# Linear attention and ternary feed-forward on eight cores: the order of three pieces of work at the end of an attention turn

## The reference

```python
# attention half: 16 heads of 64, chunks of 64 tokens, a state S carried from chunk to chunk
qkv = LN(x) @ W_qkv
k   = LN over each head's 64 values
per chunk: inter = S q;  scores = q k^T, causal;  intra = scores v;  S += v k^T;  y = inter + intra
x = x + LN(y @ W_o)
# feed-forward half: activations quantized to 8 bits by row, weights to -1, 0, 1
h = qlinear(layernorm(LN(x), gamma, beta), w1, b1);  h = gelu(h);  h = qlinear(h, w2, b2)
x = x + LN(h)
```

## Time and profile before

| | |
|---|---|
| median of three runs | 3606.48 us (3595.64 to 3606.81) |
| the profiled execution, its own time | 3602.86 us |
| its span, slowest core (core 0) | 3601.3 us (cores: 3567.2 to 3601.3) |
| busy: TensorE (PE), weight load, DVE, ACT, POOL | 58%, 29%, 43%, 20%, 4% |
| DMA | 68 GB/s over the span |

### The profile page before, as it was taken

The page is one execution under the profiler, slowest core; times in us unless marked ns, Lnnn a source line. Parts: engine busy times, 40 slices in busy tenths (PEclk is TensorE's granted clock), DMA queues, the critical chain, the costliest instruction groups (busy, mean ns, idle before and its releaser), DMA issues.

```text
span 3601.3 us, 33831 instructions; the slowest of 8 cores (3567.2 to 3601.3 us)
## 1 busy us (share of the span) xinstructions
PE 2103.5 (58%) x10640; PEld 1032.0 (29%) x10640; DVE 1538.5 (43%) x2492; ACT 726.8 (20%) x1193; POOL 145.9 (4%) x203
## 2 busy tenths in 40 slices
PE   0061566648666366647766366547776366647665
PEld 0041433413222133412222144312222233413222
DVE  0576543345543133345553133445452243355442
ACT  0030321112222111112221112212221121122221
POOL 0141300000000000000000000000000000000000
PEclk9999576669888666768887667668888676678887
DMA  9897901131111411131121311131111311031211
GB/s 186 243 196 244 173 20 31 27 102 27 41 41 27 131 27 27 24 102 27 41 41 38 123 27 24 26 113 36 27 36 38 126 26 27 23 114 33 41 30 41
DMA packets 333137, 245.50 MB, mean 68 GB/s; under 512 B 304272, under 2 KB 304288, under 8 KB 328864
## 3 DMA queue, kind: packets, MB, share of 16 engines
q0 software_dynamic: 97440, 184.58, 19.0%
q1 hardware_dynamic: 235520, 58.74, 8.8%
HBM read 159.41 MB, written 33.55 MB: 54 GB/s over the span
## 4 chain that ended last, share of the span: by engine, by line
PE 42%; DMA 22%; DVE 17%; ACT 9%; issue 7%; DVEq 1%; SPq 0%; another core or an unknown queue 0%; ACTq 0%; POOLq 0%; POOL 0%; PEldq 0%; PEld 0%
PE pb L979 14%; PE pb L897 13%; DMA abf<-abf 7%; PE pb L492 5%; DMA af<-x 4%; DMA af<-w 4%; PE pb L499 3%; DMA w2q_t<-w2qs 3%; PE pb L900 2%; DMA out<-x 1%; DMA wqkv_t<-w_qkv 1%; DVE abf L585 1%; DVE af L578 1%; ACT af L1020 1%; DVE x L740 1%
## 5 line engine op out<-in xcount | busy, mean ns | idle before, releaser
L897 PE MATMUL pb<-w1q_t,abf 128*128 128x512 fp8e4 x2048 | 541.6, 412 | 385.9 <-DMA abf<-abf 326.5
L979 PE MATMUL pb<-w2q_t,abf 128*128 128x512 fp8e4 x2048 | 499.3, 406 | 77.7 <-ACT s2rowr L968 44.4
L897 PEld LDWEIGHTS pb<-w1q_t,abf 128*128 128x128 bf16 x2048 | 190.6, 103 | 663.4 <-issue 507.3
L492 PE MATMUL pb<-abf,wqkv_t 128*128 128x128 bf16 x2048 | 188.1, 281 | 262.7 <-DMA abf<-abf 262.7
L979 PEld LDWEIGHTS pb<-w2q_t,abf 128*128 128x128 bf16 x2048 | 206.8, 103 | 352.5 <-issue 153.2
L492 PEld LDWEIGHTS pb<-abf,wqkv_t 128*128 128x128 bf16 x2048 | 183.5, 132 | 266.8 <-issue 266.8
L912 DVE TENSOR_REDUCE khs<-af 128x1 f32<-128x1024 f32 x128 | 156.1, 1220 | 174.1 <-ACT af L908 110.1
L1012 DVE RECIPROCAL scal<-scal 128x1 f32<-128x1 f32 x32 | 5.2, 164 | 473.5 <-ACT scal L1008 473.5
L908 ACT ACTIVATE af<-pb,scal 128x512 f32<-128x512 f32 x256 | 161.3, 684 | 228.8 <-PE pb L900 228.4
L528 DVE TENSOR_REDUCE khs<-pb 128x8 f32<-128x512 f32 x32 | 22.1, 692 | 433.6 <-ACT af L509 433.6
L992 ACT ACTIVATE af<-pb,scal 128x512 f32<-128x512 f32 x32 | 22.0, 687 | 560.5 <-PE pb L983 560.5
(11 more groups left out here) (162 smaller groups left out, 2766.7 us busy)
## 6 DMA issues: line engine op xcount, KB each, us to landing
af<-w POOLq DMA_DIRECT2D x16, 2048.0 KB, 9.6
wqkv_t<-qkvs POOLq DMA_DIRECT2D x3, 6144.0 KB, 22.6
af<-w POOLq DMA_DIRECT2D x32, 512.0 KB, 5.6
af<-w POOLq DMA_DIRECT2D x16, 1024.0 KB, 9.9
af<-x POOLq DMA_DIRECT2D x32, 512.0 KB, 3.8
w1q_t<-w1qs POOLq DMA_DIRECT2D x4, 4096.0 KB, 16.0
w2q_t<-w2qs POOLq DMA_DIRECT2D x4, 4096.0 KB, 25.6
out<-x POOLq DMA_DIRECT2D x32, 512.0 KB, 2.9
```

The costliest lines, as they stand in the source:

```text
L492: mi = PE.matmul(pq, lhsT=wqkv[:, kk, m * 128:(m + 1) * 128], rhs=hf[:, kk, :], start=(kk == 0), stop=(kk == 7))
L897: PE.matmul(Bk[bb0 + n2][:, :], lhsT=xf[:, kk, :], rhs=w1q[:, kk, hs0:hs0 + 512], start=(kk == 0), stop=False)
L979: mi = PE.matmul(Bk[4 + n2][:, :], lhsT=xq2_fm[:, kk, :], rhs=w2q[:, kk, n2 * 512:n2 * 512 + 512], start=(kk == 0), stop=False)
```

## The change

Three things. The two copies of v on ACT leave `a_kchain` and become `a_vevac`, called after `a_kapp_half(gg+1, 1)`, so on ACT they come behind the square root and the two normalizing operations of `a_ln2(gg)`. The addition into `x2` leaves `a_ln2` and becomes `a_x2w`, called behind the second half of k, so on DVE it comes after it. And `a_y` waits for the first half of k before its first eight heads and for the second before the other eight.

```diff
@@ a_kchain
-            A.wait_ge(s_pe, ms[f"pe_v0_{seg}_{gg}"])
-            if gg >= 1:
-                A.wait_ge(s_pe, ms[f"pe_upd_{seg}_{gg-1}"])
-            ai = A.copy(out=v_tm[:, 0:512], in_=Bk[0][:])
-            ac_mark(ai); ms[f"ac_ve0_{seg}_{gg}"] = cnt["ac"]
-            A.wait_ge(s_pe, ms[f"pe_v1_{seg}_{gg}"])
-            ai = A.copy(out=v_tm[:, 512:1024], in_=Bk[1][:])
-            ac_mark(ai); ms[f"ac_ve1_{seg}_{gg}"] = cnt["ac"]
-            ms[f"ac_ve_{seg}_{gg}"] = ms[f"ac_ve1_{seg}_{gg}"]
@@ new function, with the same nine lines
+        def a_vevac(gg):
...
@@ a_y
-            PE.wait_ge(s_dv, ms[f"dv_kln_{seg}_{gg}"])
+            PE.wait_ge(s_dv, ms[f"dv_kln0_{seg}_{gg}"])
             PE.wait_ge(s_ac, ms[f"ac_ve_{seg}_{gg}"])
...
             PE.wait_ge(s_dv, ms[f"dv_mask2_{seg}_{gg}"])
+            PE.wait_ge(s_dv, ms[f"dv_kln_{seg}_{gg}"])
@@ a_ln2, cut in two ahead of the addition into x2
+        def a_x2w(gg):
+            xb = x_tm[:, gg % 2, :]
             V.wait_ge(s_ac, ms[f"ac_ln2a_{seg}_{gg}"])
...
@@ before the loop, and in it
         a_kapp_half(0, 1)
+        a_vevac(0)
...
             a_ln2(gg)
             if gg + 1 < G:
                 a_kapp_half(gg + 1, 1)
+                a_vevac(gg + 1)
+            a_x2w(gg)
             if gg + 2 < G:
                 a_load(gg + 2)
```

More of the change, by code:

```diff
@@ L600, in a_kapp_half @@
                 ms[f"dv_kln_{seg}_{gg}"] = ms[f"dv_kln1_{seg}_{gg}"]
+        def a_vevac(gg):
+            A.wait_ge(s_pe, ms[f"pe_v0_{seg}_{gg}"])
+            if gg >= 1:
+                A.wait_ge(s_pe, ms[f"pe_upd_{seg}_{gg-1}"])
+            ai = A.copy(out=v_tm[:, 0:512], in_=Bk[0][:])
+            ac_mark(ai); ms[f"ac_ve0_{seg}_{gg}"] = cnt["ac"]
+            A.wait_ge(s_pe, ms[f"pe_v1_{seg}_{gg}"])
+            ai = A.copy(out=v_tm[:, 512:1024], in_=Bk[1][:])
+            ac_mark(ai); ms[f"ac_ve1_{seg}_{gg}"] = cnt["ac"]
+            ms[f"ac_ve_{seg}_{gg}"] = ms[f"ac_ve1_{seg}_{gg}"]
         def a_sc(gg):
```

## The result

| | before | changed kernel |
|---|---|---|
| median of 8 runs each | 3605.71 us | 3532.65 us (3519.3 to 3540.25) |
| ratio to before | | 0.9797, 95% interval 0.9779 to 0.9814 |
| profiled execution, span of its slowest core | 3601.3 us | 3531.6 us |

A forecast was written before the change was run, and what follows sets the result against it. Bound by waits: the attention turn's chain runs through k's second half, its transpose and the x load. 80.2 us gained less 5 for q's clock gives 75.2; 3527.7, adjusted halfway to the median, 3530 us, range 3512 to 3556.

The forecast's parts named there:

- The addition behind k's second half: On DVE in the attention loop: k's second half starts 2.89 us sooner each turn, 80.2 us in all.
- The addition itself doesn't move: On DVE: the addition into x2 hardly moves, starting at 1297.72 instead of 1297.62, since k's work fills its earlier wait.
- The copies of v and the waits of y cost nothing: On ACT and in y: copies behind the layernorm have 2.8 us of cover; both cost 0 and gain nothing.
- The load is released by the transpose: On POOL: the x load waits for k's transpose, the addition having 1.5 us to spare, and goes out 2.89 us sooner.
- TensorE's clock in q: In q's matmul bursts: where they fall against the clock costs +0.2 us each, +5 us, bounds -20 to +16.
- Only the mask's shift: Rival in the attention turn: only the mask's 1.48 us comes through, 3562 us; chance 0.12 together with the slower load.
- The load held by the addition: Rival at the x load: the addition ends as late as the transpose did before, 3603 to 3606 us; chance 0.04.
- A slower load in every turn: Rival at the x load: it takes 5.23 us every turn, not 3.71; 3564 us; chance 0.12 together with the mask's shift.
- A clock that stays low past q: Rival on TensorE: q, k, output projection and v all run at the low clock, 3789 us; chance 0.04.

The follow-up runs named there:

- first experiment: The kernel before with only the addition into x2 moved behind the second half of k; 3527.8 us, ratio 0.9797 to the kernel before.
- second experiment: The changed kernel with the addition put back ahead of k's second half, leaving only the copies of v and waits of y changed; 3600.6 us, ratio 1.0016.
- fourth experiment: The changed kernel with the x load no longer waiting for the transposes, only for the addition; 3474.5 us, ratio 0.9639 to the kernel before.
- seventh experiment: The changed kernel with the second statistics operation on x done twice in the 24 turns behind a load; 3528.5 us, ratio 0.9799.
- sixth experiment: The changed kernel with four x buffers, loads a turn earlier, and the front of tile gg+2 behind the state update of turn gg; 3410.0 us, ratio 0.9505.

## Why the prediction was right, point by point

- **The addition behind k's second half.** Right in place and size: 2.96 us from the second half's start (forecast 2.89), 2.93 to the load, 2.80 to the scores, 2.80 to the next q. Forecast without the clock term 80.2 us; measured on core 0, 73.5 plus the 4.9 that q took, 78.4 us, and as the mean of the cores 71.6 plus 8.6, 80.2 us. It acts alone (first experiment).
- **The addition itself doesn't move.** Right, 1.95 to 2.04 us.
- **The copies of v and the waits of y cost nothing.** Right; the copies end at 1348.99, 2.4 us before the second scores start and 3.0 before y. That nothing waited for them before was read from one row, and the second experiment confirms it.
- **The load is released by the transpose.** Right, though the profile of the changed kernel names DVE; the fourth experiment decides.
- **TensorE's clock in q.** I took +5 us. Core 0 shows +4.9 (188.1 in the earlier trace rows, now 193.0), but the mean of the cores is +8.6 (187.9 to 196.5). The working behind it was only bounds of -20 and +16 us, and the value a choice; that it hit on core 0 is luck. q did turn out to depend on the order around it, and alike on all cores: 174.7 to 196.5 us among these kernels. That what decides is where the burst falls against the clock is my reading; the seventh experiment fits it and doesn't prove it. The Trainium skill says in "TensorE: Matmul & The Clock Gate", part 1, What's actually happening, that the activity monitor runs freely. The trace agrees with this: the same burst takes from 5.00 to 6.49 us within one segment of the changed kernel. The same section puts the cost of the slow matmuls below 1% of a typical kernel's span. The 8.6 us here and the 22 us between two versions are 0.2% and 0.6% of this span, so they agree with it; beside a change of 73 us they still count.
- **The range.** Its two ends start from different numbers, 3503 from the profiled execution (3602.86 - 100) and 3542 from the median (3606.48 - 64). That is 3.6 us and changes nothing in what was forecast. Of the span, 3526 was forecast and 3531.6 measured: 1.7 us of the difference lie in the attention stages and 3.8 in the rest.
- **The rivals.** Only the mask's shift (3562 us): the scores do wait for the mask in 26 of 32 tiles, but they start 2.80 us sooner all the same, and the load leads. The load held by the addition (3603 to 3606): the addition ended at 1349.52, 2.1 us ahead of the load's issue. A slower load in every turn: the wait of the statistics for loads is unchanged (159.4 us before, 158.9 now). A clock that stays low past q: k and v kept 115.7 us each.

What stays open: what sets q. The runs show that it differs between kernels, alike on all cores, but none of them moves the burst against the clock alone, with the same work and the same gap.

## What to carry to other kernels

On an engine that works in order, look for an instruction that waits for another engine and has ready work behind it that a chain needs. To swap them shortens nothing and costs nothing, and was worth the wait plus the instruction in every turn (2.9 us x 28). Then ask what the released piece gates: here a load behind a transpose, and once both were taken out of the chain by more buffers and a front a turn ahead, a further 3% came (sixth experiment). Price a wait from its sum over the run, not from one turn.

## What the runs showed of the hardware

- The burst of q starts at 1.2 GHz in the bursts looked at (granted clock 0.50 over 3 us from 1363.8 in the changed kernel and over 2 us from 1323.35 in the sixth experiment), and the time until it rises differs from burst to burst and from kernel to kernel. The same 64 matmuls took 4.6 to 6.6 us. 18.5 us of added DVE work made the attention stages only 3.9 us longer, since q gave back 12.4. A change of 10 to 20 us in such a loop can't be put down to its edit before q is looked at.
- An `x` load of 512 KB beside a transpose disturbed neither in a way that shows: in the fourth experiment the second scores came at 5.16 us (1338.18), as in the changed kernel, and the median time of the loads from issue to landing stayed 3.8 us.
